# Cross-attention on one core: steps in groups of three over six score banks, the next batch's work moved behind the values

## The chip, the core and the metric

The kernel runs on one core of a Trainium2 chip. The metric is the device time of one launch in microseconds, from the first to the last instruction with what lies around it. Everything is fp32: products that need it are split into a high and a low part and computed with three matmuls.

## What is computed

A transformer block with cross-attention: 8 batches of 256 queries and 1601 keys, width 256, 16 heads of 16, then an MLP of inner width 1024.

```python
x = layer_norm(hidden_states, ln1_w, ln1_b)
q = (x @ q_w + q_b); k = enc @ k_w + k_b; v = enc @ v_w + v_b   # split in 16 heads
scores = einsum('bhqd,bhkd->bhqk', q, k) / sqrt(16)              # masked keys excluded
out = einsum('bhqk,bhkd->bhqd', softmax(scores), v)
hidden = out @ cproj_w + cproj_b + hidden_states
y = layer_norm(hidden, ln2_w, ln2_b)
result = hidden + gelu(y @ fc_w + fc_b) @ proj_w + proj_b
```

## The kernel before, in words

**Steps.** The 16 heads are four slots of four heads (`SLOTS`, `HG`). The 1601 keys are 13 tiles of 128 (`KT`). A step is one tile of one slot: 52 steps a batch, 416 in all. For a step TensorE computes the scores of four heads (L1140, halves of 64 rows, two heads side by side) into two PSUM banks, ScalarE takes the exponential of the 1024 columns into the buffer `pr` (L596), and TensorE multiplies them with the values and a column of ones (L1147, four heads in four column strips of the array), summed over the 13 tiles in the bank `O`. Then VectorE turns the sum (`take_o`, L806), divides (`divide`, L821 to L828), and after the fourth slot TensorE applies `cproj` (L1174).

**Row maxima.** The exponent is lowered by a maximum over a sample of keys, computed by TensorE (`max_unit`, L1127, "maximum" below) and reduced by VectorE (L787, L790). It comes back as a row of `qst`, sent by SyncE (`first_rows`, L415, from `mrow`).

**Work for the next batch.** While a batch is attended, the next one is prepared in units: eight K units (`k_unit`, products of three terms in L1077; 128 x 384 columns, the last chunk 450), 13 V units (`v_unit`, one key tile each), the transposes of x (`xt_unit`, L1106), Q (`q_unit`, L1114). A K unit is evacuated by VectorE into `kpart` (L741, L744), stored by SyncE to memory (`store_k`, L403), and from there the rows of a slot are read back into `kst` and `qst` (`first_fill`: three K loads L350, three q loads L358, one mask load L364, all from SyncE's queue). `fill_ready` holds SyncE until the stores have landed and the slot's scores of the batch before are done. The maximum of a slot waits for all seven loads (`slot_in`).

**Banks.** PSUM's eight banks are: `S` 4 (two steps), `O` 2 (the sums, and `KB` for K units and half of the maxima), `MB` 1 (the other half), `XB` 1 (V, x, Q, cproj).

**Order.** It is written out by hand for each engine. A pair p of steps (26 a batch) stands on TensorE as: scores of its two steps, the units that the tables `K_AT`, `V_AT`, `MAX_AT` and others give for p, the values of the two steps before. Scores of step n wait for the exponential of step n - 2, which had their banks. In pairs 7 and 20 a slot ends between the two values, and the units stand there. VectorE goes through the same tables. ScalarE runs the 52 exponentials in order and issues the loads of the context two batches ahead (before steps 24, 28, 32, 36), the store of V (step 48) and, in the last batch, the loads of the MLP's weights. Behind the batches stands the MLP, with the last values, division and cproj between its first products. Before them stands a head that prepares batch 0.

Of the kernel before, what the change touches and what calls it, by code (L numbers as in the profile page):

```python
# [106 lines left out]
def kb_pairs(b):  # L107

    return sorted([p for p in K_AT if b + 1 < B] + [p for p, (d, _, _) in MAX_AT.items() if b + d < B])


def mb_pairs(b):

    return sorted(p for p, (d, _, _) in MAX_AT.items() if b + d < B)


def xb_pairs(b):

    return sorted(([CPROJ_AT] if b > 0 else []) + ([XT_AT, Q_AT] + list(V_AT) if b + 1 < B else []))


def uses_before(head, pairs, b, p):

    return head + sum(len(pairs(i)) for i in range(b)) + sum(q < p for q in pairs(b))


KB_HEAD = len(HEAD_K) + len(HEAD_MAX)
MB_HEAD = len(HEAD_MAX)
XB_HEAD = KT + 2


def kb_use(b, p):
    return uses_before(KB_HEAD, kb_pairs, b, p)


def mb_use(b, p):
    return uses_before(MB_HEAD, mb_pairs, b, p)


def xb_use(b, p):  # L140
    return uses_before(XB_HEAD, xb_pairs, b, p)


def pair_of(table, what):
    return [p for p, w in table.items() if w == what][0]


XB_END = XB_HEAD + sum(len(xb_pairs(b)) for b in range(B))
MB_END = MB_HEAD + sum(len(mb_pairs(b)) for b in range(B))
KB_END = KB_HEAD + sum(len(kb_pairs(b)) for b in range(B))  # L150
# [1226 lines left out]
```

## Time and profile before

| | us |
|---|---|
| runs of the kernel before: median (lowest, highest), 3 runs | 739.46 (738.22, 741.74) |
| the profiled execution | 738.16 |
| its span, first to last instruction | 736.4 |
| TensorE busy | 690.8 (94%) |
| ScalarE busy | 446.9 (61%) |
| VectorE busy | 379.8 (52%) |
| granted TensorE clock, mean | 0.991 |

A line of the page's groups has the line of the kernel, the engine, the operation, output and inputs by their names, the count, busy time and mean duration, then the idle time in front and what ended it. PE is TensorE, PEld its weight loads, ACT ScalarE, DVE VectorE, SPq SyncE's queue. Matmuls overlap, so the time a piece of work costs TensorE is read from the start of its first matmul to the start of the next piece's first.

### The profile page before, as it was taken

How to read it: one execution, taken by the hardware profiler on the slowest of the kernel's cores; microseconds unless marked ns; L12 is line 12 of the kernel's file. 1: busy time of each engine (PE TensorE's matmuls, PEld its weight loads, DVE VectorE, ACT ScalarE, POOL GpSimd, SP SyncE). 2: the span in 40 equal slices, each digit the busy share in tenths (PEclk: the TensorE clock that was granted, in tenths of full speed). 3: DMA queues.
4: the chain of work that ended last, by engine and by line, in shares of the span. 5: the costliest groups of instructions: out<-in, count | busy, mean ns of one | idle time of the engine just before them, and what ended most of it. 6: DMA issues, size and time to landing. Idle time of an engine off the chain costs nothing.

```text
span 736.4 us, 16791 instructions
## 1 busy us (share of the span) xinstructions
PE 690.8 (94%) x7026; PEld 471.3 (64%) x7026; DVE 379.8 (52%) x848; ACT 446.9 (61%) x471; POOL 123.0 (17%) x90
## 2 busy tenths in 40 slices
PE   2579999999999999999999999999999988999997
PEld 2566665666566656665666566656665544697897
DVE  5755654554355435543555345534653372467663
ACT  5406668656865686668666765676567888622320
POOL 6222041003200320032002300230000071011010
PEclk9889999999999999999999999999999999999999
DMA  9678565446534653564456445645442700000001
GB/s 307 196 252 296 187 208 199 145 155 214 202 133 169 212 192 136 177 213 170 158 176 213 154 174 175 214 143 185 151 174 92 281 3 1 1 29 8 22 30 32
DMA packets 51082, 113.77 MB, mean 155 GB/s; under 512 B 6858, under 2 KB 39986, under 8 KB 49722
## 3 DMA queue, kind: packets, MB, share of 16 engines
q1 hardware_dynamic: 40488, 80.56, 32.5%
q10 hardware_dynamic: 10514, 32.08, 11.9%
q8 instruction: 58, 0.95, 0.5%
q14 instruction: 22, 0.18, 0.1%
HBM read 65.30 MB, written 47.06 MB: 153 GB/s over the span
## 4 chain that ended last, share of the span: by engine, by line
PE 77%; ACT 12%; DVE 5%; issue 2%; DMA 2%; ACTq 1%; DVEq 0%
PE O L1147 22%; PE S L1140 16%; ACT pr L596 12%; PE O L1077 11%; PE XB L1077 10%; PE O L1234 6%; PE S L1077 5%; PE XB L1114 2%; PE XB L1174 2%; PE MB L1127 2%; DMA k_scr<-kpart 1%; DVE kpart L741 1%; DVE kpart L744 1%; DVE g_lo L911 1%; DMA cols_s<-in_cols 1%
## 5 line engine op out<-in xcount | busy, mean ns | idle before, releaser
L596 ACT ACTIVATE pr<-S 128x1024 f32<-128x1024 f32 x416 | 400.5, 1024 | 204.2 <-PE S L1140 171.9
L1147 PE MATMUL O<-pr,vsl 128*17 128x256 f32 x3328 | 223.1, 382 | 1.3 <-DVE ot L806 1.3
L1140 PEld LDWEIGHTS S<-qst,kst 64*128 64x128 f32 x1664 | 115.0, 185 | 111.3 <-ACT pr L596 75.6
L1140 PE MATMUL S<-qst,kst 64*128 64x256 f32 x1664 | 169.6, 311 | 11.6 <-ACT pr L596 7.7
L1147 PEld LDWEIGHTS O<-pr,vsl 128*17 128x17 f32 x3328 | 74.7, 96 | 77.2 <-issue 14.9
L741 DVE TENSOR_SCALAR kpart<-O,cols_s 128x384 fp32r<-128x384 f32 x64 | 40.6, 634 | 117.2 <-PE O L1077 117.2
L528 POOL CAST c_hi<-cT 128x768 fp32r<-128x768 f32 (+1 forms) x28 | 23.9, 852 | 323.0 <-DMA cT<-in_ctx_t 170.4
L787 DVE TENSOR_REDUCE mx<-MB 128x2 fp32r<-128x512 f32 x64 | 44.1, 689 | 51.4 <-PE MB L1127 51.3
L1077 PE MATMUL O<-c_hi,w_hi 128*128 128x384 f32 (+1 forms) x128 | 52.3, 409 | 19.4 <-POOL c_lo L533 10.4
L755 DVE TENSOR_TENSOR vsl<-XB,rows_s 128x256 f32<-128x256 f32 (+1 forms) x104 | 43.3, 416 | 51.2 <-PE XB L1077 51.2
L1077 PE MATMUL XB<-w_hi,c_hi 128*128 128x256 f32 (+1 forms) x208 | 66.6, 320 | 2.9 <-DVE vsl L755 2.7
L533 POOL TENSOR_TENSOR c_lo<-cT,c_hi 128x768 fp32r<-128x768 f32 (+1 forms) x32 | 61.0, 1908 | 5.8 <-ACT c_hi L592 3.5
L1077 PE MATMUL XB<-w_lo,c_hi 128*128 128x256 f32 (+1 forms) x208 | 59.0, 284 | 0.0
L614 ACT ACTIVATE g<-S,cols_s 128x512 f32<-128x512 f32 x32 | 22.1, 690 | 60.6 <-PE S L1077 53.5
L1077 PE MATMUL XB<-w_hi,c_lo 128*128 128x256 f32 (+1 forms) x208 | 58.8, 283 | 0.0
L806 DVE STREAM_TRANSPOSE ot<-O 128x256 f32<-128x256 f32 x32 | 14.4, 450 | 73.1 <-PE O L1147 72.4
L1077 PEld LDWEIGHTS XB<-w_hi,c_hi 128*128 128x128 f32 (+1 forms) x208 | 39.0, 187 | 17.7 <-issue 8.2
L1077 PE MATMUL O<-c_lo,w_hi 128*128 128x384 f32 (+1 forms) x128 | 45.5, 355 | 0.0
L1077 PE MATMUL O<-c_hi,w_lo 128*128 128x384 f32 (+1 forms) x128 | 45.4, 355 | 0.0
L790 DVE TENSOR_REDUCE mx<-O 128x2 fp32r<-128x512 f32 x64 | 43.6, 681 | 0.0
L1077 PEld LDWEIGHTS O<-c_hi,w_hi 128*128 128x128 f32 x128 | 24.9, 194 | 28.6 <-issue 15.8
L744 DVE SCALAR_TENSOR_TENSOR kpart<-O,cols_s,kpart 128x384 fp32r<-128x384 f32 x64 | 40.6, 635 | 2.3
(96 smaller groups left out, 834.0 us busy)
## 6 DMA issues: line engine op xcount, KB each, us to landing
kst<-k_scr SPq DMA_DIRECT2D x89, 400.2 KB
k_scr<-kpart SPq DMA_DIRECT2D x48, 384.0 KB, 3.3
v_scr<-vsl ACTq DMA_DIRECT2D x8, 1768.0 KB, 6.0
cT<-in_ctx_t ACTq DMA_DIRECT2D x21, 384.0 KB, 4.7
k_scr<-kpart SPq DMA_DIRECT2D x16, 449.0 KB, 3.0
qst<-q_scr SPq DMA_DIRECT2D x87, 64.0 KB
q_scr<-qpart SPq DMA_DIRECT2D x16, 256.0 KB, 2.5
cT<-in_ctx_t ACTq DMA_DIRECT2D x7, 449.0 KB, 3.5
```

The source lines that it names most:

```text
L528: nc.gpsimd.tensor_copy(c_hi[:, c, :, 0:n], cT[:, c, :, 0:n]).then_inc(hi_done, 1)
L533: nc.gpsimd.tensor_tensor(c_lo[:, c, :, 0:n], cT[:, c, :, 0:n], c_hi[:, c, :, 0:n].bitcast(F32), ALU.subtract).then_inc(lo_done, 1)
L596: nc.scalar.activation(pr[:, n % PBUF, :], S[:, 2 * (n % 2):2 * (n % 2) + 2, :] .rearrange("p a n -> p (a n)"), ACT.Exp).then_inc(s_.exp_d ...
L741: nc.vector.tensor_scalar(kpart[:, i, 0, 0:n], KB[:, 0:n], bk_s[:, mt:mt + 1], None, ALU.add).then_inc(kh_done, 1)
L744: nc.vector.scalar_tensor_tensor(out=kpart[:, i, 1, 0:n], in0=KB[:, 0:n], scalar=bk_s[:, mt:mt + 1], in1=kpart[:, i, 0, 0:n].bitcast(F32), ...
L755: nc.vector.tensor_tensor(vsl[0:m, b % 2, :, kt, :].rearrange("p s (h w) -> p s h w", w=VW)[:, :, :, 0:HD], XB[0:m, 0:D].rearrange("p (s h ...
L787: nc.vector.tensor_reduce(mx[:, s % 2, :, j], MB[:, :].rearrange("p (q k) -> p q k", q=QT), AX.X, ALU.max, negate=True).then_inc(mb_taken, 1)
L790: nc.vector.tensor_reduce(mx[:, s % 2, :, NJ + j], KB.rearrange("p (q k) -> p q k", q=QT), AX.X, ALU.max, negate=True).then_inc(kb_taken, 1)
L1077: last = nc.tensor.matmul(dst, a, c, start=i == 0, stop=i == len(terms) - 1)
L1140: last = nc.tensor.matmul(S[:, 2 * (n % 2) + g_, j * LQ:(j + 1) * LQ], kst[rows_, s, j, kt * P:(kt + 1) * P], qst[rows_, s, j, :], start=T ...
L1147: last = nc.tensor.matmul(O[32 * h:32 * h + VW, 0, 0:LQ], vsl[:, par, s, kt, h * VW:(h + 1) * VW], pr[:, n % PBUF, h * LQ:(h + 1) * LQ], s ...
L1234: last = nc.tensor.matmul(O[:, n % 2, 0:D], w[:, i, cut], v[:, i, :], start=i == 0 and m == 0, stop=i == NI - 1 and m == 2)
```

## The change

**Groups.** The 13 steps of a slot are cut in groups of 3, 2, 3, 2, 3 (`BOUNDS`), 20 groups a batch. A group stands on TensorE as: scores of its steps, the maximum (only in groups of two, in the third pair of banks, which such a group leaves free), the values of the group before, and only then the unit. The scores of the i-th step of a group use bank pair i, and wait for the exponential of the last step that had it, or for the reduction of the maximum that had it (`emptied`). `pr` has six buffers instead of four.

**Banks.** `S` has six banks, `O` one. A single bank `U` is left for K, V, x, Q and cproj of all batches from the second on; so a unit waits until VectorE has emptied the one before. In the head, the free score banks serve for V and for every second K unit.

**Units.** Each group has at most one. V units take two key tiles (`v_pair`), seven a batch instead of 13, with the two tiles side by side in `U`. The two halves of a maximum are reduced by one VectorE instruction over 1024 columns instead of two over 512. The context's three tiles `cT`, `c_hi`, `c_lo` are laid out without gaps (`keys`), which makes room for `pr`; the instructions on them stay.

**Placing.** The wide K unit (0, 3) stands in group 7, the maximum of the next batch's slot 0 in groups 11 and 13. SyncE's queue is reordered to match. The store of V moves to step 10 of its own batch, the MLP's loads from step 4 to step 6, the transposes of y and their evacuation are split in two halves that pass through `U`.

```diff
-PBUF = 4
 STEPS = SLOTS * KT
-PAIRS = STEPS // 2
+DEEP = 3
+PBUF = 2 * DEEP
+BOUNDS = [0, 3, 5, 8, 10, KT]
+SLOTG = len(BOUNDS) - 1
+GROUPS = SLOTS * SLOTG
 SAMPLE = 256
 KBUF = 4
 CTX_AT = [24, 28, 32, 36]
 
 
...
-K_AT = {0: (0, 0), 2: (0, 1), 4: (0, 2), 6: (0, 3), 8: (1, 0), 10: (1, 1), 12: (1, 2), 14: (1, 3)}
-V_AT = {0: 0, 1: 1, 6: 2, 7: 3, 9: 4, 11: 5, 12: 6, 13: 7, 15: 8, 16: 9, 18: 10, 20: 11, 22: 12}
-MAX_AT = {3: (0, 2, 0), 5: (0, 2, 1), 9: (0, 3, 0), 11: (0, 3, 1),
-          15: (1, 0, 0), 17: (1, 0, 1), 21: (1, 1, 0), 23: (1, 1, 1)}
-DIV_AT = {1: SLOTS - 1, 8: 0, 14: 1, 21: 2}
-CPROJ_AT, XT_AT, Q_AT = 3, 4, 5
-XSUMS_AT = {6 + i: 2 * QT + i for i in range(TOK - 2 * QT)}
-YN_AT, YT_AT = 13, 16
-STRADDLE = (7, 20)
+K_AT = {0: (0, 0), 1: (0, 1), 5: (0, 2), 7: (0, 3), 9: (1, 0), 10: (1, 1), 12: (1, 2), 14: (1, 3)}
+V_AT = {6: 0, 8: 1, 11: 2, 15: 3, 16: 4, 17: 5, 19: 6}
+CPROJ_AT, XT_AT, Q_AT = 2, 3, 4
+XSUMS_AT = {4 + i: 2 * QT + i for i in range(TOK - 2 * QT)}
+YN_AT, YT_AT = 13, 14
 BLK = 32
 QBLK = LQ // BLK
 
 HEAD_K = [(mt, c) for mt in range(2) for c in range(CH)]
 HEAD_MAX = [(s, j) for s in range(2) for j in range(NJ)]
...
+def steps_of(g):
+
+    s, k = divmod(g, SLOTG)
+    return range(KT * s + BOUNDS[k], KT * s + BOUNDS[k + 1])
+
...
+def max_of(b, g):
+
+    s, k = divmod(g, SLOTG)
+    b_, s_ = b + (s + 2) // SLOTS, (s + 2) % SLOTS
+    return (b_, s_, k // 2) if len(steps_of(g)) < DEEP and b_ < B else None
+
...
-        S = stack.enter_context(nc.psum_tensor("S", [P, 4, 512], F32))
-        O = stack.enter_context(nc.psum_tensor("O", [P, 2, 512], F32))
-        MB = stack.enter_context(nc.psum_tensor("MB", [P, 512], F32))
-        XB = stack.enter_context(nc.psum_tensor("XB", [P, 512], F32))
-        KB = O[:, 1, :]
+        S = stack.enter_context(nc.psum_tensor("S", [P, 2 * DEEP, 512], F32))
+        O = stack.enter_context(nc.psum_tensor("O", [P, 512], F32))
+        U = stack.enter_context(nc.psum_tensor("U", [P, 512], F32))
...
                 first_fill(sp, b, 3)
                 if b + 1 < B:
-                    for c in range(3):
-                        store_k(b + 1, 0, c)
+                    store_k(b + 1, 0, 0)
+                    store_k(b + 1, 0, 1)
                 first_rows(b, 2)
                 if b + 1 < B:
                     store_q(b + 1)
+                    store_k(b + 1, 0, 2)
                     store_k(b + 1, 0, 3)
                     first_fill(sp, b + 1, 0)
+                first_rows(b, 3)
+                if b + 1 < B:
                     store_k(b + 1, 1, 0)
                     store_k(b + 1, 1, 1)
-                first_rows(b, 3)
-                if b + 1 < B:
+                    first_fill(sp, b + 1, 1)
                     store_k(b + 1, 1, 2)
-                    first_fill(sp, b + 1, 1)
+                    first_rows(b + 1, 0)
                     store_k(b + 1, 1, 3)
-                    first_rows(b + 1, 0)
                     first_fill(sp, b + 1, 2)
                     first_rows(b + 1, 1)
...
+            def v_pair(b, i):
+                bank_free(u_taken, v_use(b, 2 * i))
+                for t, kt in enumerate(tiles_of(i)):
+                    last = v_products(b, kt, U[:, t * D:(t + 1) * D])
+                last.then_inc(u_ready, 1)
...
+            def emptied(b, g, i):
+
+                for at in range(GROUPS * b + g - 1, -1, -1):
+                    b_, g_ = divmod(at, GROUPS)
+                    if i < len(steps_of(g_)):
+                        return pe.wait_ge(first.exp_done, STEPS * b_ + steps_of(g_)[i] + 1)
+                    if max_of(b_, g_):
+                        return pe.wait_ge(peak_taken, max_use(b_, g_) + 1)
...
+
+            def scores(b, g):
+                for i, n in enumerate(steps_of(g)):
+                    s, kt = divmod(n, KT)
+                    if kt == 0:
+                        pe.wait_ge(first.mrow_in[s], ROWS_IN * (b + 1))
+                    emptied(b, g, i)
+                    score_products(s, kt, i).then_inc(first.scores_done, 1)
 
...
-                for p in range(PAIRS):
-                    for n in (2 * p, 2 * p + 1):
-                        scores(b, n)
-                    before = [(b, n - 2) if n >= 2 else (b - 1, STEPS + n - 2) for n in (2 * p, 2 * p + 1)]
-                    if p in STRADDLE:
-                        values(*before[0])
-                        units(b, p)
-                        values(*before[1])
-                    else:
-                        units(b, p)
-                        if before[0][0] >= 0:
-                            for of_batch, n in before:
-                                values(of_batch, n)
-            values(B - 1, STEPS - 2)
+                for at in range(GROUPS):
+                    scores(b, at)
+                    if max_of(b, at):
+                        emptied(b, at, DEEP - 1)
+                        max_unit(*max_of(b, at), DEEP - 1)
+                    if at > 0:
+                        for n in steps_of(at - 1):
+                            values(b, n)
+                    elif b > 0:
+                        for n in steps_of(GROUPS - 1):
+                            values(b - 1, n)
+                    units(b, at)
+            for n in steps_of(GROUPS - 1)[:-1]:
+                values(B - 1, n)
```

TensorE before, in pair 9 of a middle batch: values of pair 7's steps (L1147), scores (L1140), the two halves of a maximum (L1127, into `MB` and `KB`), a V unit (L1077), values.

```order
L1147 MATMUL O<-pr,vsl 17x256 x8
L1140 MATMUL S<-qst,kst 128x256 x8
L1127 MATMUL MB<-kst,qst 128x256
L1127 MATMUL O<-kst,qst 128x256
L1127 MATMUL MB<-kst,qst 128x256
L1127 MATMUL O<-kst,qst 128x256
L1077 MATMUL XB<-w_hi,c_hi 128x256
L1077 MATMUL XB<-w_lo,c_hi 128x256
L1077 MATMUL XB<-w_hi,c_lo 128x256
L1077 MATMUL XB<-w_hi,c_hi 128x256
L1077 MATMUL XB<-w_lo,c_hi 128x256
L1077 MATMUL XB<-w_hi,c_lo 128x256
```

TensorE after, groups 13 and 14: scores of two steps and maximum (L1179, L1167, `S`), values of three steps (L1186), scores of three, values of two, the wide K unit (L1106), scores.

```order
L1179 MATMUL S<-qst,kst 128x256 x8
L1167 MATMUL S<-kst,qst 128x256 x4
L1186 MATMUL O<-pr,vsl 17x256 x12
L1179 MATMUL S<-qst,kst 128x256 x12
L1186 MATMUL O<-pr,vsl 17x256 x8
L1106 MATMUL U<-c_hi,w_hi 128x450
L1106 MATMUL U<-c_lo,w_hi 128x450
L1106 MATMUL U<-c_hi,w_lo 128x450
L1106 MATMUL U<-c_hi,w_hi 128x450
L1106 MATMUL U<-c_lo,w_hi 128x450
L1106 MATMUL U<-c_hi,w_lo 128x450
L1179 MATMUL S<-qst,kst 128x256 x12
```

The values now follow on the scores or the maximum, the unit stands behind them, and the next scores follow on the unit. In group 13 there is no unit.

SyncE's queue before, from the first K stores of the next batch on: K stores, rows of maxima of slot 2 (L415), q stores (L409), the wide K store, the fill of slot 0 (L350, L358, L364).

```order
L403 DMA k_scr<-kpart 128x2x384 [waits kb_taken] x3
L415 DMA qst<-mrow 1x4x64 [waits mrow_done]
L415 DMA qst<-mrow 1x4x64 x3
L409 DMA q_scr<-qpart 128x2x256 [waits ql_done]
L409 DMA q_scr<-qpart 128x2x256
L403 DMA k_scr<-kpart 128x2x449 [waits kb_taken]
L350 DMA kst<-k_scr 32x2x1601 [waits k_out2,k_out3,k_out1,first_scores_done,k_out0,q_out]
L350 DMA kst<-k_scr 32x2x1601 x2
L358 DMA qst<-q_scr 32x512 x3
L364 DMA kst<-mask_scr 2x2x1601
L403 DMA k_scr<-kpart 128x2x384 [waits kb_taken] x2
L415 DMA qst<-mrow 1x4x64 [waits mrow_done]
```

SyncE's queue after, the same stretch.

```order
L423 DMA k_scr<-kpart 128x2x384 [waits u_taken] x2
L435 DMA qst<-mrow 1x4x64 [waits mrow_done]
L435 DMA qst<-mrow 1x4x64 x3
L429 DMA q_scr<-qpart 128x2x256 [waits ql_done]
L429 DMA q_scr<-qpart 128x2x256
L423 DMA k_scr<-kpart 128x2x384 [waits u_taken]
L423 DMA k_scr<-kpart 128x2x449 [waits u_taken]
L370 DMA kst<-k_scr 32x2x1601 [waits k_out2,k_out3,k_out1,first_scores_done,k_out0,q_out]
L370 DMA kst<-k_scr 32x2x1601 x2
L378 DMA qst<-q_scr 32x512 x3
L384 DMA kst<-mask_scr 2x2x1601
L435 DMA qst<-mrow 1x4x64 [waits mrow_done]
```

Two K stores stand in front of the rows of slot 2 instead of three; the third went behind the q stores. Behind the fill of slot 0 come the rows of slot 3 at once, where two K stores stood.

## Rows read from the trace of the kernel before

**Rows 1.** The page: engines, the chain by engine, one group of VectorE

```profile
PE 690.8 (94%) x7026; PEld 471.3 (64%) x7026; DVE 379.8 (52%) x848; ACT 446.9 (61%) x471; POOL 123.0 (17%) x90
...
PE 77%; ACT 12%; DVE 5%; issue 2%; DMA 2%; ACTq 1%; DVEq 0%
...
L787 DVE TENSOR_REDUCE mx<-MB 128x2 fp32r<-128x512 f32 x64 | 44.1, 689 | 51.4 <-PE MB L1127 51.3
```

**Rows 2.** Busy time by stage; length, PE, PEld, DVE, ACT, POOL, clock, DMA

```profile
56.04:128.43 72.39, 70.78 (x779) 45.73 (x778) 40.92 (x109) 49.52 (x52) 15.35 (x11) 1.00 0.63 224
...
277.00:351.28 74.28, 73.35 (x806) 47.50 (x802) 35.85 (x78) 50.17 (x53) 12.40 (x9) 1.00 0.51 177
...
574.46:632.74 58.28, 52.41 (x669) 27.99 (x665) 23.19 (x62) 50.97 (x55) 15.35 (x5) 1.00 0.17 63
632.74:736.36 103.62, 96.98 (x622) 86.14 (x618) 64.32 (x136) 27.34 (x40) 7.18 (x3) 0.99 0.07 22
```

**Rows 3.** Waits within 574.46 to 632.74: total us, times, longest us

```profile
PEld S L1140 <- ACT pr L596: 12.6, 27, 1.3
```

**Rows 4.** The chain in order of time, 280 to 370: start us, us

```profile
287.60 1.92 PE XB L1174 x8
...
292.42 0.44 PE XB L1106 x4
...
298.41 1.44 PE O L1077 x6
299.84 0.71 PE XB L1077 x6
300.56 0.99 PE O L1147 x16
301.54 0.67 PE S L1140 x8
302.21 0.56 PE O L1147 x8
302.77 0.91 PE XB L1077 x6
...
304.91 1.25 PE O L1077 x6
```

**Rows 5.** Timeline of PE, 329 to 346: start us, us, line

```profile
330.77 0.73 PE L1140 MATMUL S<-qst,kst 64*128 64x256 f32 x8
...
331.34 0.28 PE L1127 MATMUL MB<-kst,qst 63*128 63x256 f32 x1
...
331.67 1.06 PE L1147 MATMUL O<-pr,vsl 128*17 128x256 f32 x16
...
337.28 0.50 PE L1140 MATMUL S<-qst,kst 64*128 64x256 f32 x4
...
338.16 0.50 PE L1140 MATMUL S<-qst,kst 64*128 64x256 f32 x4 [0.38 <-ACT pr L596]
...
338.60 0.63 PE L1147 MATMUL O<-pr,vsl 128*17 128x256 f32 x8
```

**Rows 6.** Timeline of SyncE's queue, 296 to 313, fill of slot 0

```profile
304.16 1.89 SPq L350 DMA_DIRECT2D kst<-k_scr  x3
...
308.01 0.58 SPq L364 DMA_DIRECT2D kst<-mask_scr  x1
```

**Rows 7.** DMA by microsecond: length, clock, busy share of DMA engines, GB/s

```profile
310.00:311.00 1.00, 1.00 0.96 353
311.00:312.00 1.00, 1.00 0.21 69
```

**Rows 8.** Timeline of PE, 56 to 62: V unit, then scores

```profile
55.84 0.28 PE L1077 MATMUL XB<-w_hi,c_lo 128*65 128x256 f32 x1
56.04 0.74 PE L1140 MATMUL S<-qst,kst 64*128 64x256 f32 x8
```

**Rows 9.** Timeline of ACT, 47 to 62: first four exponentials

```profile
58.10 3.77 ACT L596 ACTIVATE pr<-S 128x1024 f32<-128x1024 f32 x4 [31.14 <-issue]
```

More of the change, by code:

```diff
@@ L100 @@
 HEAD_MAX = [(s, j) for s in range(2) for j in range(NJ)]
+HEAD_X = ["v0", "v1", "v2", "xt", "q"] + [f"v{t}" for t in range(3, KT)]
 class Section:
     pass
[L107 to L124, printed above, removed]
@@ L127 @@
[L127 to L150, printed above, removed]
@@ L155, in k_use, with u_groups, u_use, max_use @@
+def u_groups(b):
+    return sorted(([CPROJ_AT] if b > 0 else []) + ([XT_AT, Q_AT] + list(K_AT) + list(V_AT) if b + 1 < B else []))
+def u_use(b, g):
+    return len(HEAD_K) + sum(len(u_groups(i)) for i in range(b)) + sum(q < g for q in u_groups(b))
+def max_use(b, g):
+    return len(HEAD_MAX) + sum(max_of(*divmod(i, GROUPS)) is not None for i in range(GROUPS * b + g))
+def group_of(table, what):
+    return [g for g, w in table.items() if w == what][0]
+U_END = u_use(B, 0)
 def k_use(b, mt, c):
-    return HEAD_K.index((mt, c)) if b == 0 else kb_use(b - 1, pair_of(K_AT, (mt, c)))
+    return HEAD_K.index((mt, c)) if b == 0 else u_use(b - 1, group_of(K_AT, (mt, c)))
@@ L256, in build, with keys @@
         qf, xT = xn, attT
+        def keys(t, c, n):
+            return t[:, :, T0[c] * P:T0[c] * P + n]
         late = ExitStack()
@@ L673, in _ @@
                     for n in range(STEPS):
-                        exponential(whole, b, n)
+                        exponential_again(b, n)
                 y_t(whole, 0)
@@ new lines, in v_pair_evac, with xt_evac @@
+            def v_pair_evac(b, i):
+                dve.wait_ge(pads_set, 10)
+                if i == 0 and b >= 2:
+                    dve.wait_ge(v_out, 16 * (b - 1))
+                dve.wait_ge(u_ready, v_use(b, 2 * i) + 1)
+                for t, kt in enumerate(tiles_of(i)):
+                    last = v_tile(b, kt, U[:, t * D:(t + 1) * D])
+                last.then_inc(u_taken, 1)
+            def xt_evac(b, use):
+                bank, ready, taken = x_bank(b)
+                dve.wait_ge(ready, use + 1)
@@ L1096, in v_unit @@
                 pe.wait_ge(lo_done, CH * b + c + 1)
-                bank_free(xb_taken, v_use(b, kt))
-                product3(XB[0:m, 0:D], [(c_hi[:, c, k, cut], c_lo[:, c, k, cut]) for k in range(KC)],
-                         [(w_hi[:, 1, k, :], w_lo[:, 1, k, :]) for k in range(KC)]).then_inc(xb_ready, 1)
+                return product3(bank[0:m, :], [(keys(c_hi, c, NKE[c])[:, k, cut], keys(c_lo, c, NKE[c])[:, k, cut])
+                                               for k in range(KC)],
+                                [(w_hi[:, 1, k, :], w_lo[:, 1, k, :]) for k in range(KC)])
@@ L1118, in max_unit @@
[L1118 removed]
+                last.then_inc(ready, 1)
+            def max_unit(b, s, j, i):
                 if j == 0:
                     pe.wait_ge(first.slot_in[s], 16 * FILLS * (b + 1))
[L1122 to L1123 removed]
                 for q in range(QT):
[L1125 removed]
+                    for g_ in range(2):
                         rows_ = slice(g_ * HALF, g_ * HALF + MAXROW)
[L1127 removed]
+                        last = nc.tensor.matmul(S[:, 2 * i + g_, q * SAMPLE:(q + 1) * SAMPLE], query_set(rows_, s, j, q),
@@ L1301, in _ @@
-            values(B - 1, STEPS - 2)
+                if g in K_AT and more:
+                    k_unit(b + 1, *K_AT[g])
+                if g == CPROJ_AT and b > 0:
+                    cproj(b - 1, u_use(b, g))
+                if g == XT_AT and more:
+                    xt_unit(b + 1, u_use(b, g))
+                if g == Q_AT and more:
+                    q_unit(b + 1, u_use(b, g))
+                if g in V_AT and more:
+                    v_pair(b + 1, V_AT[g])
+                if b == B - 1 and g == YT_AT:
+                    pe.wait_ge(u_taken, u_use(b, g))
+                    turn_y(first, 0, [0])
@@ new lines, in units @@
+                if b == B - 1 and g == YT_AT + 1:
+                    pe.wait_ge(first.yt_done, 1)
+                    turn_y(first, 0, [1])
+            for b in range(B):
+                for at in range(GROUPS):
+                    scores(b, at)
[8 more added lines that the diff above has]
+                            values(b - 1, n)
+                    units(b, at)
```

388 lines of the change are left out of this document (188 added, 200 removed).

## The prediction

> **What bounds the kernel now.** I read the page first. TensorE is busy for 94% of the span, and the chain that ended last runs 77% through it and 12% through ScalarE's exponentials [rows 1]. Then I cut the span at the first score matmul of each batch. The reader is to see three kinds of stage [rows 2]: six middle batches of 74.3 to 74.6 us (one is shown), the last batch (58.28 us, ScalarE busy in 50.97 of them), and 103.62 us of MLP behind them. In a middle batch TensorE reads 73.35 of 74.28 us busy, and ScalarE 50.17. So TensorE sets the pace there, and a saving must come from its own sequence. In the last batch, which computes nothing for a next one, both engines have gaps and wait for each other [rows 3].
>
> What does TensorE do with 74.28 us? I price its pieces by the distance to the next piece's start. Values of two steps take 0.99, of one step 0.56, so a step is 0.43 and a start 0.13 [rows 4]. Scores of two steps take 0.67 before values, 0.57 before a maximum, and a maximum before values 0.33 [rows 4, 5]. A K unit takes 1.25, the wide one (450 keys) 1.44; a V unit alone 0.91, behind a K unit 0.71 [rows 4]. So it costs 0.20 to turn the array to full-width units. A batch of before is then: values 24 x 0.99 + 4 x 0.56 = 26.0; scores 18 x 0.67 + 8 x 0.57 = 16.6; maxima 8 x 0.33 = 2.6; K 6 x 1.25 + 2 x 1.44 = 10.4; V 10 x 0.91 + 3 x 0.71 = 11.2; transposes of x behind a K unit 0.44; cproj 1.92 [rows 4], and Q, the same matmuls, as much. Sum 71.1. The remaining 3.1 us are TensorE's waits for a score bank. One is shown whole: scores that began at 337.28 were cut in two by an exponential, and took 1.32 instead of 0.67 [rows 5].
>
> **The change, part by part.**
>
> *Scores and values in groups of 3, 2, 3, 2, 3 steps.* Four slots give 12 groups of three and 8 of two. Values: 12 x 1.42 + 8 x 0.99 = 25.0, 1.0 less. Three-step scores: one step alone takes 0.44 (338.16 to 338.60 [rows 5]), two take 0.67, so three take 0.90; with eight two-step groups, all followed by a maximum, 12 x 0.90 + 8 x 0.57 = 15.4, 1.2 less.
>
> *Units behind the values.* The maximum stays behind the scores (same 64-row halves), K, V, q and the rest go behind the values. K units no longer stand beside a V unit: 10.4 as before. V units become pairs of tiles: six at 0.91 + 0.71 = 1.62, the short one 0.91, together 10.6 instead of 11.2. The transposes lose their K unit: 0.64. Sum of after: 25.0 + 15.4 + 2.6 + 10.4 + 10.6 + 0.6 + 3.8 = 68.4, or 2.7 less than the 71.1.
>
> *A price the batches of before do not show* is scores right behind a full-width unit; there values always stood in front. The nearest row is the one such place in the head: the last V matmul at 55.84, scores at 56.04 [rows 8], 0.20 and thus no more than V to values. Lower bound nothing, upper bound another 0.20 for each of 18 units, 3.6 us a batch. I take nothing, by that row.
>
> *The waits for a bank.* Exponentials follow each other every 3.77 / 4 = 0.94 us [rows 9] and start some 0.5 us after their scores do (one step's 0.44 and the handover). After a three-step group the third bank pair is free at 0.5 + 2.8 = 3.3. TensorE wants it again, for a maximum, after 0.90 + 0.99 + 1.25 + 0.57 = 3.7. The two-step groups that have no unit behind them ask for the reduced bank: scores 0.57, maximum 0.33, then VectorE's reduction of twice 689 ns [rows 1], 2.4; asked for at 0.57 + 0.33 + 1.42 + 0.46 = 2.8. Only the short V unit in front of a new batch leaves a gap, 0.90 + 0.99 + 0.91 + 0.46 = 3.26 against 3.3: 0.1 to 0.2. The 3.1 us go; I put 0.2 in their place. What hides the exponentials is the unit behind the values; without it (last batch) the wait stays.
>
> *What is late next: the fill of slot 0.* The next batch's K and q rows go through memory and back into kst. Their last K unit now stands in group 7 and the maximum that reads them in group 11; before it was pair 6 and pair 15. From the wide K unit at 298.41 to the first load of the fill is 5.8 us (evacuation, store, its landing); SyncE issues seven loads until 308.6; the DMA engines' share is 0.96 until 311 and 0.21 in the next microsecond [rows 4, 6, 7]. So landed is 13.3 us after the unit's start. TensorE now gets from there to the maximum in 1.44 + (0.57 + 0.33 + 1.42 + 1.62) + (0.90 + 0.99 + 1.25) + (0.90 + 1.42 + 1.25) + 0.57 = 12.7 us. It waits 0.6 us, with values and a V pair queued behind, in each of seven batches. SyncE itself is not behind: the other fills and the rows of maxima have 4 or more groups to spare.
>
> A middle batch: 68.4 + 0.2 + 0.6 = 69.2 against 74.28, so 5.0 less; six of them 30.2.
>
> *First batch.* Its start is not TensorE's: ScalarE, still issuing loads, starts its first exponential at 58.10, the third ends at 60.9 [rows 9], and group 1's maximum waits for it, to 61.0. (Two K banks in the head buy nothing for that reason.) Behind it: 68.4 less cproj 1.9, less one values group 1.42, less the pieces already done 0.90 + 1.25 + 0.57, is 62.4, plus 0.6: it ends at 124.0 instead of 128.43. 4.4 less.
>
> *Last batch.* TensorE's pieces are some 45 us, so ScalarE bounds it: 50.97 busy, plus the gaps that remain. These are 0.5 at the start, 0.5 at each of four maxima (0.33 and 1.42 of values end after two exponentials), 1.3 at cproj, 0.1 at the others: 4 us. 55 instead of 58.28: 3.3 less. MLP: same matmuls, other banks; nothing.
>
> Sum: 30.2 + 4.4 + 3.3 = 37.9 us off the profiled execution's own 738.16 us (span 736.4): 700.3. The median of the runs shown is 1.3 above that execution, so I say 701.
>
> **The rivals.**
>
> *The fill of slot 0 comes later still (18%).* ScalarE issues the load of the next chunk of ctx before step 24, now 7 us behind the wide K unit, inside the fill; before, six pairs stood between. The load is 128 x 768 floats, 0.39 MB, and the DMA engines moved 353 GB/s when full [rows 7]: up to 1.1 us more if it goes ahead of the fill's packets, 8 us in seven batches; with a slower store beside it twice that. 709 to 717. Against it: SyncE's issuing, not bandwidth, sets 4.4 of the fill's 7.5 us [rows 6]. The Trainium skill (DMA: Bandwidth & Descriptors, "Issuing engines are not separate DMA queues") says that transfers issued by different engines share the same 16 DMA engines and interleave. By that rule the wait grows by this 1.1 us; no row of before has both transfers in the fill of slot 0.
>
> *Exponentials still gate the scores (15%).* My margins are 0.1 to 0.4 us. If ScalarE starts 0.5 us later than I think (two queues of DMA issues stand between its exponentials), twelve groups of three lose 0.3 us each, 3 us a batch: the change would remove the waits only in name, and 701 + 21 x 0.6 to 701 + 21 is 714 to 722. For it: 12.6 us of such waits in the last batch [rows 3]. Against it: in the middle batches ScalarE is idle a third of the time [rows 2].
>
> *No wait for the fill at all (12%).* If SyncE or TensorE is 0.6 us off, 696.
>
> *Slower than before (4%).* One mechanism: the fill of slot 0 read in group 11. Every microsecond it is late costs seven. Four groups are 12.7 us; from a landing 6 us later than now (19 us behind the unit) the gain of 38 is gone. It would need SyncE held at a wait in front of the fill, for instance for the maxima's rows of slot 2, which stand before the q and K stores. These rows are ready in group 3, four groups earlier, so I give it little.
>
> **How the numbers follow.** The forecast has 51%, with 697 to 706 as its own range. With the rivals, 690 to 716 leaves out less than 2 in 10: the low end takes in no fill wait and cheaper joints, the high end the late fill and most of the upper bound of the joint. A change of 0.5% is about what this measurement can tell from none. Faster by more than that 0.94, within it 0.03, slower 0.03.
>
> **What would show it right or wrong.** A middle batch of 69 us between first score matmuls. No wait of TensorE's score weights for the exponential above 0.3 us there; in each batch one wait of the maximum's weights for the mask or q load of slot 0, 0.3 to 1.5 us. Scores of three steps at 0.90 and values at 1.42, also behind a unit. The last batch at 55 us, ScalarE nearly without gaps. I am wrong if scores behind a unit cost 0.2 more, if maxima wait over 2 us, or if the MLP moves by more than 1 us.

## The result, and the profile after

The changed kernel takes 730.06 us (median of 4 runs, 726.19 to 731.76); the kernel before took 738.84 us in the same comparison (738.20 to 741.74). The ratio is 0.9863, with a 95% interval of 0.9839 to 0.9886. It is faster by 1.4%, where I had forecast 5% and 701 us; 730 lies outside my range of 690 to 716. The profiled run took 730.79 us, its span 729.0.

The page of after, beside [rows 1] (the third row is a group of VectorE: busy, mean ns of one, idle before and what ended it):

```profile
PE 670.8 (92%) x7026; PEld 474.5 (65%) x7026; DVE 373.1 (51%) x784; ACT 443.3 (61%) x471; POOL 122.5 (17%) x90
...
PE 76%; DVE 7%; DMA 7%; ACT 5%; SPq 2%; issue 2%; ACTq 0%; DVEq 0%
...
L825 DVE TENSOR_REDUCE mx<-S 128x4 fp32r<-128x1024 f32 x64 | 77.8, 1216 | 18.3 <-PE S L1167 18.2
```

TensorE is busy for 20 us less, and the chain holds 5% of ScalarE instead of 12%. The waits of the score weights for the exponential, in one middle batch of before (277.00 to 351.28) and then in all six of after (132 to 565; us in total, times, longest):

```profile
PEld S L1140 <- ACT pr L596: 8.9, 22, 0.6
```

```profile
PEld S L1179 <- ACT pr L618: 4.2, 18, 0.3
```

That is three short waits a batch instead of 22, so the exponentials have left the path as forecast. But DMA has gone from 2% to 7% of the chain. The same cut by stage as in [rows 2], at the first score matmul of each batch (length, then PE, PEld, DVE, ACT, POOL busy, granted clock, DMA share, GB/s):

```profile
58.44:132.06 73.62, 70.56 (x770) 47.91 (x770) 38.30 (x98) 49.35 (x52) 10.51 (x8) 0.93 0.52 180
132.06:204.26 72.20, 70.35 (x805) 47.46 (x804) 35.00 (x71) 49.48 (x53) 12.33 (x9) 0.98 0.53 183
204.26:279.50 75.24, 70.55 (x803) 47.30 (x802) 34.84 (x70) 49.69 (x53) 12.34 (x9) 0.98 0.52 176
279.50:350.24 70.74, 68.94 (x805) 46.78 (x804) 34.84 (x70) 49.69 (x53) 12.33 (x9) 1.00 0.53 186
350.24:422.72 72.48, 70.60 (x805) 47.47 (x804) 34.85 (x70) 49.70 (x53) 12.32 (x9) 0.98 0.53 182
...
565.44:625.70 60.26, 51.96 (x673) 29.32 (x673) 24.25 (x59) 50.73 (x55) 15.19 (x5) 0.94 0.25 91
625.70:729.00 103.30, 96.92 (x622) 86.09 (x618) 64.27 (x136) 27.28 (x40) 7.16 (x3) 0.99 0.06 22
```

Three things are to be seen. Where the clock is 1.00, TensorE's busy time is 68.94, close to the 68.6 that I had summed from pieces, but the batch takes 70.74: 1.8 us are a wait. In the three batches where the clock is 0.98, busy time itself is 1.4 to 1.7 us more. And the last batch has become 2 us longer than before, not 3.3 shorter.

**The wait.** The waits over the whole of after, then SyncE's queue, ScalarE's and TensorE in the second batch (start, length, idle before and what ended it):

```profile
PE S L1167 <- DMA kst<-mask_scr: 16.1, 5, 4.7
```

```profile
162.26 0.37 SPq L423 DMA_DIRECT2D k_scr<-kpart  x1
165.05 1.91 SPq L370 DMA_DIRECT2D kst<-k_scr  x3
167.00 1.87 SPq L378 DMA_DIRECT2D qst<-q_scr  x3
168.91 0.58 SPq L384 DMA_DIRECT2D kst<-mask_scr  x1
```

```profile
165.14 0.39 ACTq L363 DMA_DIRECT2D cT<-in_ctx_t  x1
...
168.52 0.38 ACTq L363 DMA_DIRECT2D cT<-in_ctx_t  x1
```

```profile
159.22 0.47 PE L1106 MATMUL U<-c_hi,w_hi 128*128 128x450 f32 x1
...
171.32 0.73 PE L1179 MATMUL S<-qst,kst 64*128 64x256 f32 x8
173.90 0.51 PE L1167 MATMUL S<-kst,qst 63*128 63x256 f32 x4 [1.85 <-ACT pr L618]
174.34 2.71 PE L1186 MATMUL O<-pr,vsl 128*17 128x256 f32 x24
```

The wide K unit starts at 159.22, the first load of the fill is issued 5.8 us later as before, the last one at 168.91, and the maximum of group 11 starts at 173.90. Its scores began 2.58 us ahead of it, where 0.58 is their price: 2.0 us of wait. (The row puts the idle time down to ScalarE; the last landing of slot 0's fill, at 173.76 by the landings in the trace, is the later of the two.) In seven batches this maximum waits 2.6, 2.0, 4.85, 1.95, 2.04, 2.84 and 2.27 us, together 18.5; I had said 0.6 each, 4.2. The fill landed 14.5 to 17.4 us behind the wide unit, not 13.3. Inside six of the seven ScalarE issued two loads of ctx, 5.9 and 9.3 us behind the unit; in the last, which landed after 14.8 us, none.

**The clock.** Behind the wait the values take 2.71 us where the same 24 matmuls take 1.49 elsewhere. The granted clock fell from 2.4 GHz to half (1.2 GHz) at this wait in four of the seven batches (waits of 2.6, 2.0, 4.85 and 2.04 us): in the last us of it in the first batch, just behind it in the others. It stayed there for 6.8 us in the first batch and for 3.4 in the three others. Two batches with waits of the same length tell its price: after 1.95 us the clock stayed at 1.00 and the batch took 70.74; after 2.04 it fell and the batch took 72.48. That is 1.7 us for a stretch of 3.4 us.

**The last batch.** VectorE and GpSimd there:

```profile
584.91 3.20 DVE L729 TENSOR_SCALAR rs<-rs 128x14 int32<-128x14 int32 x1
588.15 4.47 DVE L731 TENSOR_SCALAR rs<-rs 128x14 int32<-128x14 int32 x1
...
594.53 1.23 DVE L825 TENSOR_REDUCE mx<-S 128x4 fp32r<-128x1024 f32 x1
```

```profile
583.51 4.57 POOL L581 TENSOR_TENSOR fc_lo<-fc_raw,fc_hi 128x2048 fp32r<-128x2048 f32 x1
588.02 4.58 POOL L582 TENSOR_TENSOR pj_lo<-pj_raw,pj_hi 128x2048 fp32r<-128x2048 f32 x1
```

```profile
590.31 0.74 PE L1179 MATMUL S<-qst,kst 64*128 64x256 f32 x8
595.81 0.80 PE L1179 MATMUL S<-qst,kst 64*128 64x256 f32 x4 [4.77 <-DVE mx L825]
```

Two operations on 14 columns take 3.20 and 4.47 us. The first ends at 588.11, when GpSimd's first subtraction ends (588.08); the second at 592.62, with GpSimd's second (592.60). The reduction of group 8 stands behind them and holds the score banks: 12 score matmuls that take 0.91 elsewhere reach from 590.31 to 596.54. The change had moved this inverse root of the LayerNorm to group 7. In before it ran behind the subtractions, at 602.75, and the two operations took 0.13 and 0.17 us.

The ledger, by the spans of the profiled runs; the last column is the kernel E3 below, in which two numbers of the change are set otherwise:

| stage | before | forecast | after | E3 |
|---|---|---|---|---|
| head and first batch | 128.43 | 124.0 | 132.06 | 127.89 |
| six middle batches | 446.03 | 415.8 | 433.38 | 413.18 |
| last batch | 58.28 | 55.0 | 60.26 | 53.94 |
| MLP | 103.62 | 103.6 | 103.30 | 103.29 |
| span | 736.4 | 698.4 | 729.0 | 698.3 |

### The profile page after: what moved, and what is told of

Same layout as the page of the kernel before. It is cut to its first block, busy times and chain, and to the rows that moved or that the text cites. A ratio compares the mean times of both kernels' runs of the same rounds, so it can differ in the third digit from the quotient of the medians.

```text
span 729.0 us, 16705 instructions
## 1 busy us (share of the span) xinstructions
PE 670.8 (92%) x7026; PEld 474.5 (65%) x7026; DVE 373.1 (51%) x784; ACT 443.3 (61%) x471; POOL 122.5 (17%) x90
## 3 DMA queue, kind: packets, MB, share of 16 engines
q10 hardware_dynamic: 10514, 32.08, 12.7%
## 4 chain that ended last, share of the span: by engine, by line
PE 76%; DVE 7%; DMA 7%; ACT 5%; SPq 2%; issue 2%; ACTq 0%; DVEq 0%
PE O L1186 24%; PE U L1106 18%; PE S L1179 15%; PE S L1106 6%; ACT pr L618 4%; DMA kst<-mask_scr 4%; PE U L1285 3%; PE O L1285 3%; PE S L1167 3%; PE U L1226 2%; DMA k_scr<-kpart 2%; PE U L1156 2%; SPq L378 1%; SPq L370 1%; DVE g_lo L946 1%
## 5 line engine op out<-in xcount | busy, mean ns | idle before, releaser
L1186 PE MATMUL O<-pr,vsl 128*17 128x256 f32 x3328 | 217.1, 390 | 0.0
L1179 PE MATMUL S<-qst,kst 64*128 64x256 f32 x1664 | 147.3, 303 | 8.5 <-DVE mx L825 4.8
L1179 PEld LDWEIGHTS S<-qst,kst 64*128 64x128 f32 x1664 | 110.9, 188 | 53.6 <-issue 29.7
L1186 PEld LDWEIGHTS O<-pr,vsl 128*17 128x17 f32 x3328 | 82.6, 98 | 75.2 <-issue 5.8
L825 DVE TENSOR_REDUCE mx<-S 128x4 fp32r<-128x1024 f32 x64 | 77.8, 1216 | 18.3 <-PE S L1167 18.2
L768 DVE TENSOR_SCALAR kpart<-U,cols_s 128x384 fp32r<-128x384 f32 (+1 forms) x60 | 38.0, 633 | 92.2 <-PE U L1106 92.2
L777 DVE TENSOR_TENSOR vsl<-U,rows_s 128x256 f32<-128x256 f32 (+1 forms) x91 | 34.7, 419 | 86.5 <-PE U L1106 86.4
L1106 PE MATMUL U<-c_hi,w_hi 128*128 128x384 f32 (+1 forms) x120 | 48.8, 407 | 10.4 <-POOL c_lo L554 10.4
L1106 PE MATMUL U<-w_hi,c_hi 128*128 128x256 f32 (+1 forms) x182 | 57.1, 314 | 0.0
L1106 PE MATMUL U<-w_lo,c_hi 128*128 128x256 f32 (+1 forms) x182 | 52.0, 286 | 0.0
L1106 PE MATMUL U<-w_hi,c_lo 128*128 128x256 f32 (+1 forms) x182 | 51.9, 285 | 0.0
L1167 PE MATMUL S<-kst,qst 63*128 63x256 f32 x256 | 28.6, 301 | 22.7 <-DMA kst<-mask_scr 16.1
L1106 PEld LDWEIGHTS U<-w_hi,c_hi 128*128 128x128 f32 (+1 forms) x182 | 34.6, 190 | 22.4 <-issue 22.4
L1106 PEld LDWEIGHTS U<-c_hi,w_hi 128*128 128x128 f32 x120 | 23.3, 194 | 34.2 <-issue 33.9
L841 DVE STREAM_TRANSPOSE ot<-O 128x256 f32<-128x256 f32 x32 | 14.4, 449 | 58.8 <-PE O L1186 58.0
L1106 PE MATMUL U<-c_hi,w_lo 128*128 128x384 f32 (+1 forms) x120 | 42.9, 357 | 0.0
L1106 PE MATMUL U<-c_lo,w_hi 128*128 128x384 f32 (+1 forms) x120 | 42.8, 356 | 0.0
L771 DVE SCALAR_TENSOR_TENSOR kpart<-U,cols_s,kpart 128x384 fp32r<-128x384 f32 (+1 forms) x60 | 38.0, 633 | 2.1
```

Source lines behind the costliest of these rows:

```text
L768: nc.vector.tensor_scalar(kpart[:, i, 0, 0:n], k_room(b, use)[:, 0:n], bk_s[:, mt:mt + 1], None, ALU.add).then_inc(kh_done, 1)
L771: nc.vector.scalar_tensor_tensor(out=kpart[:, i, 1, 0:n], in0=k_room(b, use)[:, 0:n], scalar=bk_s[:, mt:mt + 1], in1=kpart[:, i, 0, 0:n].b ...
L777: return nc.vector.tensor_tensor(vsl[0:m, b % 2, :, kt, :].rearrange("p s (h w) -> p s h w", w=VW)[:, :, :, 0:HD], bank[0:m, :].rearrange( ...
L825: nc.vector.tensor_reduce(mx[:, s % 2, :, j:HG:NJ].rearrange("p q g -> p g q"), S[:, 2 * i:2 * i + 2, :].rearrange("p g (q k) -> p g q k", ...
L1106: last = nc.tensor.matmul(dst, a, c, start=i == 0, stop=i == len(terms) - 1)
L1167: last = nc.tensor.matmul(S[:, 2 * i + g_, q * SAMPLE:(q + 1) * SAMPLE], query_set(rows_, s, j, q), kst[rows_, s, j, q * SAMPLE:(q + 1) * ...
```

## The experiments

The kernel before ran beside them, at 739.73 us (E1 to E4), 741.01 (E5 to E8) and 739.55 (E9, E10). Each diff is against the changed kernel unless another is named.

**E1: the fill of slot 0 one group earlier.**

```
-K_AT = {... 7: (0, 3), ...}   V_AT = {6: 0, ...}
+K_AT = {... 6: (0, 3), ...}   V_AT = {7: 0, ...}
```

> The changed kernel with one thing moved: the wide K unit (0, 3) from group 7 to group 6, the V pair of tiles 0 and 1 from 6 to 7. The work is the same. Theory (fill): in the changed kernel the maximum in group 11 waited 2.0 to 4.9 us for the fill of slot 0 in each of seven batches, 18.5 us in all, and after four of these waits the granted clock stood at the half level, which cost some 1.7 us a time and more in batch 0, 7 us in all. One group earlier is 3.9 us more time, so the waits go and the clock stays up: 18 + 7 less than 730, 705 (702 to 709), middle batches at 69.0. Rival (another wait is right behind): if the fill only hides a second wait, the reduction, the exponentials or slot 2's fill, middle batches stay above 70.5 and the time above 714. Rival (the clock falls by itself, not after waits): the clock rows at half level stay as many, and the time is 712.

Measured: 707.34 us (705.73 to 708.68), ratio 0.9556 [0.9521, 0.9591]. The third batch, and the waits of the whole kernel:

```profile
196.82:265.53 68.71, 68.71 (x803) 46.67 (x803) 34.95 (x70) 49.70 (x53) 12.32 (x9) 1.00 0.56 192
```

```profile
PE S L1167 <- DMA kst<-mask_scr: 2.9, 2, 2.6
```

TensorE is busy for the whole batch. The middle batches take 68.44 to 69.35 us, some 23 us come back by moving one K unit past one V unit (TensorE now takes 16.2 us from the wide unit to the maximum instead of 12.7), and no middle batch has a half-clock stretch. The last batch (61.09) is untouched. So the wait and the clock behind it are one cause, and it is shown.

**E2: the inverse root of the last batch at group 12.**

```
-                if b == B - 1 and g == 7:
+                if b == B - 1 and g == 12:
```

> The changed kernel, with the inverse root of the MLP's layer norm on VectorE in the last batch moved from group 7 to group 12. Theory: in the changed kernel its two first instructions (14 int32 columns) took 3.20 and 4.47 us instead of 0.13 and 0.17, and ended at the moment at which GpSimd's two large subtractions ended; the reduction of the maximum of group 8 stood behind them, and the scores of group 9 waited 5.3 us for the bank, then ran at half clock for 6.8 us. Moved, the wait goes: 5.3 + 2 less, 723 (721 to 725). Rival: the last batch is bound by ScalarE, which makes the 5 us good later: 729.

Measured: 723.49 us (718.17 to 725.36), ratio 0.9762 [0.9707, 0.9818]. The last batch takes 53.95 us instead of 60.26, and L729 takes 132 ns there.

**E3: both.**

> Both moves together. Theory: the two losses are apart in time and add, 25 + 7 less than 730: 698 (694 to 702), which is what was forecast for the change itself (701). Rival (second waits): above 710. A head that stays at 58.4 us (before: 56.0) and a last batch of 53 to 55 us are expected by both.

Measured: 699.68 us (696.55 to 700.10), ratio 0.944 [0.9403, 0.9477]. Its stages are in the ledger. The two moves give back 30.4 us, so two terms and what follows from them are the difference to the measured 730; that is shown. That the time also meets my 701 is in part luck: E3's head and first batch end 3.9 us later than forecast, and against this stand the wait of 0.6 us a batch, which this kernel hardly has any more, and a last batch 1.1 us shorter than forecast.

**E4 and E7: ctx loads later, the K unit left at group 7.** Two steps, since E4 took one load out of the fill and left the next one in it, 9.3 us behind the wide unit.

```
-CTX_AT = [24, 28, 32, 36]
+CTX_AT = [28, 32, 36, 40]     (E4)
+CTX_AT = [32, 35, 38, 41]     (E7)
```

> The changed kernel with the context loads of ScalarE's queue before steps 28, 32, 36, 40 instead of 24, 28, 32, 36; the wide K unit stays in group 7. Theory (the load goes through the same DMA engines as the fill): the landing of slot 0's fill after its mask load's issue falls from 4.5 to 5.0 us to the 3.0 to 3.7 of the kernel before, each wait by 1.3 us, seven of them, and with shorter waits fewer spells of half clock: 9 to 14 less, 716 to 721. Rival (the fill is slower for another reason, its own 1.2 MB or SyncE's issuing): landing stays at 4.5 and more, 729.

> The changed kernel with the context loads before steps 32, 35, 38, 41, so that none is issued while TensorE waits for the fill; the wide K unit stays in group 7. With the loads before 24 and 28, two of them (0.39 MB each) ran within the fill; before 28 and 32 one still ran at its end. Theory (the fill shares the DMA engines with the context loads): the fill lands 13.3 us after the wide K unit's start instead of 14.5 and more, the wait in group 11 falls from 2.0 to 0.8 us and less varied, and spells of half clock get rare: 730 less 7 x 1.6 less 7, 712 (708 to 718). Rival (what lengthens the fill's end is SyncE's own traffic behind it, rows of maxima and K stores): landing stays at 14.3, 726 as with the earlier move.

Measured: E4 725.98 us (720.65 to 728.96), ratio 0.9785 [0.9735, 0.9835], a miss: the fill still landed 13.9 to 16.3 us behind the unit. E7 715.41 us (715.05 to 716.84), ratio 0.9649 [0.96, 0.9698]: landed 12.9 to 15.2 us behind it, waits 0.36 to 2.7 us, 9.1 in all. Its second batch beside after's 72.20:

```profile
128.44:198.89 70.45, 68.72 (x803) 46.72 (x803) 34.98 (x71) 49.47 (x53) 12.35 (x9) 1.00 0.56 187
```

So the ctx loads made about half of the 18.5 us of waits, and with the clock most of the 15 us between the changed kernel and E7. Five of the six fills that had them landed 1.0 to 2.2 us earlier without them; the one of the second batch did not (14.54 and 14.42 us). The other half is the fill itself, which without them lands up to 2 us later than the single one that I had priced. A rival for this half was not tested: SyncE's own transfers behind the fill have changed too. Before, one K store was issued between the mask load at 308.01 and the landing; in the changed kernel four rows of slot 3 and two K stores were, from 169.54 on.

**E5: GpSimd's work later, VectorE's left at group 7.** A second way to part the two: if the root in group 7 were wrong for another reason, this would not help.

```
-                    if n == 6 and b + 1 == B:
+                    if n == 15 and b + 1 == B:
                         load_mlp()
```

> The changed kernel with the MLP's weight loads issued before step 15 of the last batch instead of 6; VectorE's inverse root stays in group 7. GpSimd's two large subtractions then run some 12 us later and no longer beside it. Theory (the two small int32 instructions stood still while GpSimd's subtraction ran): they take 0.13 and 0.17 us, scores of group 9 wait for nothing, the last batch takes 54 instead of 60.3 us, 723. Rival (they are slow for their own reason, type or place): 3.2 and 4.5 us as before, 730. A wait of the normalisation for GpSimd in group 13 may take up to 2 us of it.

Measured: 722.18 us (721.12 to 726.37), ratio 0.9759 [0.9701, 0.9818]; the last batch takes 53.95. All L729 and L731 on 14 columns, of E5 and then of after:

```profile
L731 DVE TENSOR_SCALAR rs<-rs 128x14 int32<-128x14 int32 x1 | 0.2, 176 | 0.0
...
L729 DVE TENSOR_SCALAR rs<-rs 128x14 int32<-128x14 int32 x1 | 0.2, 165 | 0.0
```

```profile
L731 DVE TENSOR_SCALAR rs<-rs 128x14 int32<-128x14 int32 x1 | 4.5, 4474 | 0.0
L729 DVE TENSOR_SCALAR rs<-rs 128x14 int32<-128x14 int32 x1 | 3.2, 3202 | 0.0
```

Same instructions, same place, 165 and 176 ns once GpSimd's subtractions are elsewhere. It is the meeting of the two that costs.

**E6: is it the order within a group?** E3 with the unit in front of the values on TensorE.

```
+                units(b, at)
                 if at > 0:
                     for n in steps_of(at - 1):
                         values(b, n)
                 ...
-                units(b, at)
```

> The kernel with both moves (699.7 us), and the units again between the scores (or the maximum) and the values, as in the kernel before; groups, banks, pairs of V tiles stay. Theory (the place of the unit costs TensorE the same either way; groups and V pairs are what saves): middle batches 68.7 + 8 x 0.1 for maxima in front of a unit, 69.2; 700 to 705. Rival (that the values follow directly on the scores is what removes the waits for exponentials): middle batches above 71, 714 and more.

Measured: 724.53 us (721.71 to 725.0), ratio 0.9761 [0.9708, 0.9814], a miss by my theory, and the number of the rival. The middle batches take 72.25 us (one of them 72.62) instead of E3's 68.4 to 69.6, at full clock. But the rival's mechanism, waits for exponentials, isn't what is seen. A place with its wait, TensorE and then VectorE:

```profile
298.22 0.41 PE L1167 MATMUL S<-kst,qst 63*128 63x256 f32 x4
299.63 0.44 PE L1106 MATMUL U<-c_hi,w_hi 128*128 128x450 f32 x1 [1.00 <-DVE kpart L771]
```

```profile
297.88 0.45 DVE L841 STREAM_TRANSPOSE ot<-O 128x256 f32<-128x256 f32 x1 [2.37 <-PE O L1186]
298.25 0.57 DVE L768 TENSOR_SCALAR kpart<-U,cols_s 128x384 fp32r<-128x384 f32 x1
298.86 0.62 DVE L771 SCALAR_TENSOR_TENSOR kpart<-U,cols_s,kpart 128x384 fp32r<-128x384 f32 x1
```

TensorE waits for the one unit bank, not for an exponential. VectorE empties it late: the take of a slot's output (L841) stands in front of the evacuation and waits for values, which now come behind the unit.

**E10: E6 with VectorE's order turned as well.**

```
-                if k == 0 and (b > 0 or s > 0):
-                    take_o(b if s > 0 else b - 1, (s - 1) % SLOTS)
                 if g in K_AT and more:
                     k_evac(b + 1, *K_AT[g])
                 ...
+                if k == 0 and (b > 0 or s > 0):
+                    take_o(b if s > 0 else b - 1, (s - 1) % SLOTS)
```

> The kernel with units before values on TensorE (724.5, middle batches 72.25), and on VectorE the evacuation of the unit now in front of the take of the slot's output. My theory: 724.5 came from the one unit bank, which VectorE emptied late since the take of the slot's output, in front of it in its queue, waits for values that now stand behind the unit; with the order on VectorE turned as well, middle batches come back to 68.5 to 70 and the time to 700 to 707. Rival (units before values cost this by themselves: the unit bank is asked for again too soon behind the maximum, or exponentials gate the scores once no unit stands between values and scores): middle batches stay at 71.5 to 72.5, 720 to 725.

Measured: 699.44 us (698.07 to 701.93), ratio 0.946 [0.9433, 0.9486]. All 25 us are back, and the third batch is full:

```profile
196.30:265.01 68.71, 68.71 (x806) 46.68 (x803) 35.38 (x70) 49.69 (x53) 12.30 (x10) 1.00 0.57 193
```

So in the middle batches units in front of the values or behind them are worth the same; the last batch takes 55.37 us here and 53.94 in E3. What counts is that the engine that empties the bank meets its work in TensorE's order. The score weights of this kernel wait for exponentials just as those of E6 do, 48 times and 18.8 us in the middle batches, 0.4 us at most, and its batches are full all the same: such short waits of PEld cost TensorE nothing here.

**E8: the head's waits filled.** E3 with 40 and 16 matmuls, whose result nothing reads, in front of the maxima of slots 0 and 1.

```
+            def fill_time(count):
+                pe.wait_ge(u_taken, len(HEAD_K))
+                for i in range(count):
+                    nc.tensor.matmul(U[:, 0:D], w_hi[:, 0, 0, 0:P], w_hi[:, 1, 0, :], start=True, stop=True)
```

> The kernel with both moves (699.7 us), and 40 and 16 extra products of 256 columns into the free bank U where TensorE waits in the head for the fills of slots 0 and 1; their results are never read. Theory (the half clock from 39.6 to 63.5 us follows on TensorE's waits in the head): the spell gets shorter or goes, batch 0 takes 66 instead of 68.4 us, and its start moves from 59.5 to 57: 695 (693 to 698). Rival (the clock falls in the head whatever TensorE does, or the start is set by the loads): 699 to 702, since the extra products cost what they take.

Measured: 698.49 us (697.17 to 700.47), ratio 0.9426 [0.9375, 0.9478]. The head's last two stretches in E8, then in E3:

```profile
40.00:50.00 10.00, 8.53 (x67) 7.74 (x66) 3.95 (x7) 0.00 (x0) 2.34 (x3) 1.00 0.96 342
50.00:58.80 8.80, 5.69 (x44) 4.78 (x44) 4.55 (x9) 0.00 (x0) 2.93 (x3) 1.00 0.57 189
```

```profile
40.00:50.00 10.00, 4.14 (x19) 3.47 (x20) 2.57 (x3) 0.00 (x0) 1.56 (x2) 0.50 0.99 345
50.00:59.50 9.50, 6.77 (x31) 5.14 (x30) 4.90 (x9) 0.00 (x0) 3.17 (x3) 0.50 0.56 186
```

The clock stays whole, and in the profile the first batch ends at 126.32 instead of 127.89. In the times this is inside the scatter: the intervals overlap, and a gain isn't shown. Nor is the clock safe with it: E9 has the same extra matmuls, and its clock was at half from 58.4 to 65.2 us.

**E9: all together.** E8 with E7's CTX_AT.

> The last K unit of slot 0 in group 6, the inverse root of the last batch in group 12, ctx loads of ScalarE at steps 32, 35, 38, 41, and 56 matmuls whose result nothing reads in the head's waits. My theory: the fill of slot 0 has a group more, the ctx loads are behind it, VectorE's root stands behind GpSimd's long subtractions; so no batch waits for a fill: middle batches 68.4 to 68.8, last batch 54, head and first batch 126.3 together: 697 us, ratio 0.943. Rival (ctx loads that come later delay the sums of the next batch, or the rows for which they are read): a middle batch above 69.5, 703 or more.

Measured: 697.37 us (696.13 to 699.46, 5 runs), ratio 0.9431 [0.9412, 0.945]. It beats the kernel before by 5.7% and the changed one by 33 us. Against E3 and E8 it can't be told apart: with the K unit in group 6 the fill has time enough, and the ctx loads no longer matter.

## Why the prediction was wrong, point by point

**The step that failed** is "what is late next: the fill of slot 0", its term of 0.6 us a batch. The place and the mechanism were right; the size was 1.95 to 4.85 us, 18.5 in seven batches where I had 4.2. I took the landing from one fill of before, 13.3 us, and set it against TensorE's 12.7. Before, such fills landed 12.7 to 14.1 us behind the unit in the trace. With a margin below zero, every later landing counts in full. I priced the ctx load beside it in a rival, as 1.1 us for one load; there were two in the fill's time, and E7 shows what taking them away gives: about 1.3 us a batch. In the Trainium skill (DMA: Bandwidth & Descriptors, "Issuing engines are not separate DMA queues") transfers of different engines share the 16 DMA engines. By that rule the rival should have been the forecast; E7 agrees with it in five fills of six. The rest of the step, up to 2 us by which the fill lands late without those loads, stays open. One fill, that of the third batch (75.24 us), was issued 8.4 us behind its unit instead of 5.8, since the last part of the store in front of it landed 8.2 us behind the unit instead of 5.7. The same batch is the slowest in E2, E4, E5 and E7; why, stays open.

**A term that was missing: the clock behind a wait.** I let a wait cost its own length. Four of seven came with half the clock: three for 3.4 us at 1.7 us each, the one of the first batch for twice as long, which by the same measure is some 3.4 us (an estimate). The rivals missed this too: the two loads made 9.4 us of waits, and E7, without them, is 14.7 us faster.

**A term that was missing: VectorE beside GpSimd.** I counted the moved inverse root at nothing and didn't ask what GpSimd does in group 7. [rows 2] shows GpSimd busy for 15.35 us in the last batch, and this was the place to look. The cost is 6.3 us (60.26 against 53.95 in E2 and E5): 5.3 of wait for the score bank, and the rest goes with the half clock from 594.3 to 601.1. The Trainium skill has the mechanism (SBUF — State Buffer, "SBUF: two separate sides"): some VectorE operations share a pair of ports with GpSimd, whoever starts first holds it for its whole instruction, and the other stands still. The trace agrees to 0.03 us: both operations end with GpSimd's. It also shows that the reduction from PSUM, which started at 583.77 beside the same subtraction, took its usual 1.23.

**The head.** I had left it alone. Its maximum of slot 0 is reached earlier and waits for the fill at half clock; the first batch starts at 58.44 instead of 56.04. Of the 5.7 us by which that batch missed its forecast, 2.0 are the fill's wait; the other 3.7 go with two half-clock stretches (granted clock 0.93), above all the one of 6.8 us behind the wait, since E3's first batch, at half clock only in its first 4 us, takes 68.41. The start itself moves from run to run with the same head: 56.51 in E4, 59.74 in E2. Why, stays open.

**What held.** The pieces, as medians over the middle batches: scores of three steps 0.908 (forecast 0.90), values 1.420 (1.42) and 0.988 (0.99), a V pair 1.610 (1.62), K 1.263 and 1.423 (1.25, 1.44), scores in front of a maximum 0.574 to 0.584 (0.57), the maximum 0.332 (0.33), the transposes 0.587 (0.64). Scores right behind a full-width unit cost nothing, the value I chose between nothing and 3.6 us a batch. The exponentials gate nothing in a middle batch. But I had put this down to the unit behind the values, and E10 does as well with the unit in front of them, so its place isn't the reason. How much of the gain is due to the groups over six banks and how much to the pairs of V tiles was not tested apart; only the sum of the pieces speaks for my split. Without the term for the fill my middle batch is 68.6 us, and E1 has 68.71; for the last batch I had 55, and E2 has 53.95.

**The rivals.** "The fill comes later still" (18%) was the right one by its mechanism, but it ended at 717, since it knew neither the clock nor the last batch. With 8.5 us for the clock and the 5.3 by which the last batch missed its forecast, its 709 to 717 would have been 723 to 731; this is reckoned with hindsight. "Exponentials still gate" was wrong: even in E6, where no unit stands between values and scores, TensorE waited for a bank of VectorE's. "No wait for the fill" and "Slower than before" were wrong too: the fill landed at most 17.4 us behind the unit, where the second needed 19.

## What to carry to other kernels

Where a regrouping brings a producer and its reader closer, price the transfer by its slowest case in the trace, list every other queue's transfers in that time, and leave a margin: here one group, 3.5 us, was worth 23 us. A wait of TensorE of 2 us can cost nearly double, since the clock may fall behind it. When a step moves on one engine, write beside it what the other engines do at its new place; and turn the order of the engine that empties a bank together with the one that fills it.

## What the runs showed of the hardware

- Two int32 operations of VectorE on 14 columns stood still for 3.20 and 4.47 us until GpSimd's subtraction ended, and took 0.165 and 0.176 us with GpSimd elsewhere (E5). A reduction from PSUM beside the same subtraction was not held.
- The granted clock fell to half at waits of 2.0, 2.04, 2.6 and 4.85 us in the changed kernel, and not after those of 1.95, 2.27 and 2.84; in E7 only at the longest (2.7). In E4 and E5 it fell at waits of 1.66, 1.81 and 1.85 us too, and did not at one of 3.4 (the first batch of E5). The length of the wait alone doesn't decide, and what else does stays open.
- A fill through memory, six loads and a mask, landed 12.9 to 17.4 us behind the unit that makes its rows (E7 and the changed kernel): the spread alone is longer than a group.
